# Scores of the second layer from block-diagonal keys, in one 128-row product of 512 columns for each query half

## What is computed

```python
def attention(q, k, v, mask):                 # for each batch and head
    scores = einsum('bqhd,bkhd->bhqk', q, k) * scale      # 256 x 256 for each head
    p = softmax(where(mask, -big, scores))
    return einsum('bhqk,bkhd->bqhd', p, v)
x = layernorm(x + attention(xWq, cWk, cWv) Wo)            # layer 0: "A", heads of 64
x = layernorm(x + attention(xWq, xWk, xWv) Wo)            # layer 1: "B", heads of 16
x = layernorm(x + attention(xWq, cWk, cWv) Wo)            # layer 1: "C", heads of 16
x = layernorm(x + relu(x W1) W2)
```

## Time and profile before

| | us |
|---|---|
| median of 3 runs | 1829.49 (1823.51 to 1831.89) |
| span of the profiled execution | 1832.3 |
| PE busy | 1728.2 (94% of the span) |
| PE weight loads | 1295.4 (71%) |
| DVE busy | 1280.9 (70%) |
| ACT busy | 1189.8 (65%) |
| POOL busy | 988.2 (54%) |
| mean busy share of the 16 DMA engines over the main queue's packets | 54.6% |
| granted clock of TensorE, mean | 0.986 |

### The profile page before, as it was taken

The page is one execution under the profiler, slowest core; times in us unless marked ns, Lnnn a source line. Parts: engine busy times, 40 slices in busy tenths (PEclk is TensorE's granted clock), DMA queues, the critical chain, the costliest instruction groups (busy, mean ns, idle before and its releaser), DMA issues.

```text
span 1832.3 us, 37274 instructions
## 1 busy us (share of the span) xinstructions
PE 1728.2 (94%) x11456; PEld 1295.4 (71%) x11456; DVE 1280.9 (70%) x4810; ACT 1189.8 (65%) x3985; POOL 988.2 (54%) x1030
## 2 busy tenths in 40 slices
PE   8698999999989999999999999999999999998887
PEld 6576777777767777777777777777776777775556
DVE  4265767776867867687776768677776867667763
ACT  4264676767666676776666677766767676566752
POOL 2244554647546464755646475554646555454742
PEclk9899999999999999999999999999999999999999
DMA  8421416575665857567585756758575675614110
GB/s 160 120 93 65 145 43 224 161 242 174 210 229 163 284 165 235 187 205 241 171 279 159 239 181 209 240 174 284 170 247 156 214 231 174 214 34 150 43 58 13
DMA packets 223171, 319.95 MB, mean 175 GB/s; under 512 B 31488, under 2 KB 192000, under 8 KB 214784
## 3 DMA queue, kind: packets, MB, share of 16 engines
q1 hardware_dynamic: 219856, 317.55, 54.6%
q10 hardware_dynamic: 3120, 0.01, 0.1%
HBM read 166.49 MB, written 151.00 MB: 173 GB/s over the span
## 4 chain that ended last, share of the span: by engine, by line
PE 77%; DMA 6%; DVE 6%; SPq 4%; ACT 4%; issue 2%; POOL 0%; POOLq 0%; DVEq 0%
PE ps_g L671 45%; PE ps_t L820 10%; PE ps_t L843 8%; PE ps_s L796 8%; PE ps_av L796 3%; DMA prob_b<-p_kept 3%; ACT prob L926 3%; PE ps_av L843 3%; DMA p_kept<-blocks 2%; DVE prob L1103 2%; PE ps_g L677 1%; SPq L584 1%; DVE res_ln L1079 1%; DMA x_tok<-x 1%; DVE prob_b L1134 1%
## 5 line engine op out<-in xcount | busy, mean ns | idle before, releaser
L1227 POOL TENSOR_TENSOR prob<-prob,recip 128x512 f32<-128x512 f32 x768 | 785.9, 1045 | 676.4 <-DVE recip L1113 671.5
L926 ACT ACTIVATE prob<-prob,ext 128x256 f32<-128x256 f32 x1536 | 757.2, 499 | 13.9 <-DVE ext L1103 13.4
L936 ACT ACTIVATE prob_t<-ps_t 128x512 f32<-128x512 f32 x384 | 226.4, 593 | 406.5 <-PE ps_t L820 405.6
L820 PE MATMUL ps_t<-ident,prob 128*128 128x128 f32 x1920 | 304.7, 284 | 7.0 <-DVE prob_b L1134 5.7
L926 ACT ACTIVATION_READ_ACCUMULATOR prob<-prob,ext 128x1 f32 x1536 | 295.0, 192 | 0.0
L820 PEld LDWEIGHTS ps_t<-ident,prob 128*128 128x128 f32 x1920 | 217.7, 142 | 92.7 <-issue 51.9
L1103 DVE CUSTOM_DVE_ANT_0 prob<-ps_s,mask_a 128x256 f32<-128x256 f32 x392 | 145.3, 421 | 87.3 <-PE ps_s L796 70.4
L1125 DVE STREAM_TRANSPOSE blocks<-prob 128x512 f32<-128x512 f32 x288 | 183.8, 676 | 2.3 <-POOL prob L1227 2.2
L1103 DVE CUSTOM_DVE_ANT_0 prob<-ps_s,zero 128x256 f32<-128x256 f32 x392 | 144.4, 418 | 49.8 <-PE ps_av L796 42.0
L1103 DVE CUSTOM_DVE_ANT_0 prob<-ps_s,mask_b 128x256 f32<-128x256 f32 x368 | 136.0, 417 | 24.1 <-PE ps_s L796 14.0
L796 PE MATMUL ps_s<-k_ctx,q 64*128 64x256 f32 x784 | 144.8, 402 | 5.8 <-DVE ext L1103 2.2
(11 more groups left out here) (122 smaller groups left out, 3022.6 us busy)
## 6 DMA issues: line engine op xcount, KB each, us to landing
p_kept<-blocks SPq DMA_DIRECT2D x576, 128.0 KB, 2.4
prob_b<-p_kept SPq DMA_DIRECT2D x144, 512.0 KB, 3.3
k_parts_C<-k_hl SPq DMA_DIRECT2D x64, 256.0 KB, 3.2
k_parts_B<-k_hl SPq DMA_DIRECT2D x64, 256.0 KB, 3.0
q_parts_B<-q_hl SPq DMA_DIRECT2D x64, 256.0 KB, 3.5
k_B<-k_parts_B SPq DMA_DIRECT2D x16, 1024.0 KB, 7.8
q_B<-q_parts_B SPq DMA_DIRECT2D x16, 1024.0 KB, 7.8
q_parts_C<-k_hl SPq DMA_DIRECT2D x64, 256.0 KB, 4.8
```

The source lines that it names most:

```text
L820: last = nc.tensor.transpose(two(ps_t[e])[:, kt, qt * P:(qt + 1) * P], src[:, e, qt, kt * P:(kt + 1) * P], ident[:, :])
L926: last = nc.scalar.activation(tile, tile, ACT.Exp, bias=ext[:, slot, e, t:t + 1], scale=-1.0, accum_out=sums[:, slot, e, t:t + 1])
L936: nc.scalar.activation(prob_t[:, e], two(ps_t[e]), ACT.Copy).then_inc(copied_second, 1)
L1227: nc.gpsimd.tensor_tensor(rows, rows, recip[:, slot, e].unsqueeze(2) .to_broadcast([P, TT, TOK]), ALU.mult).then_inc(normed[s], 1)
```

## The change

The keys of B and C get a second index: k4 is [128, 2, 8, 256] instead of [128, 8, 256]. Slice e holds head e's keys in rows 64e to 64e+63 and zeros in the other 64 rows, so the two slices side by side are block-diagonal. One product of 128 rows and 512 columns with the queries of half t gives both heads' scores of that half, in one PSUM bank. So there are two products for a pair instead of four, and a bank now holds a query half (both heads) instead of a head (both halves). DVE and ACT follow the new order for B and C; for A nothing is changed. The zeros are written once, by four memsets on DVE at the start, with a semaphore that PE waits for. The keys are read back with two DMAs of 64 partitions instead of one of 128, and the semaphore counts go from 16 to 32 with it. To make room in SBUF, the program's scratch for dynamic DMAs is set to 1024 bytes.

```diff
-        k4 = {s: sb("k4_" + s, [P, PAIRS, TOK], F32R) for s in "BC"}
+        k4 = {s: sb("k4_" + s, [P, 2, PAIRS, TOK], F32R) for s in "BC"}
@@ save_keys
-                    sp.wait_ge(spread_k["B"], count(b - 1, 16, 16))
+                    sp.wait_ge(spread_k["B"], count(b - 1, 32, 32))
@@ spread_keys
-                rows = "e a r c t -> (e a r) c t" if s == "B" else "b e a r c t -> (b e a r) c t"
-                sp.dma_start(k4[home][:, :, :].bitcast(F32), kept.rearrange(rows)).then_inc(spread_k[s], 16)
+                rows = "e a r c t -> e (a r) c t" if s == "B" else "b e a r c t -> e (b a r) c t"
+                for e in range(2):
+                    sp.dma_start(k4[home][HALF * e:HALF * (e + 1), e].bitcast(F32), kept.rearrange(rows)[e]
+                                 ).then_inc(spread_k[s], 16)
@@ scores
-                    pe.wait_ge(spread_k[s], count(b, 16, 16))
+                    pe.wait_ge(halves_cleared, 1)
+                    pe.wait_ge(spread_k[s], count(b, 32, 32))
-                    q, k = q4[home][:, place(p), :], k4[home][:, place(p), :]
+                    q, k = q4[home][:, place(p), :], k4[home][:, :, place(p), :]
+                if s != "A":
+                    for t in range(TT):
+                        nc.tensor.matmul(two(score_bank(body, step, t)), q[:, t * P:(t + 1) * P], k,
+                                         start=True, stop=True).then_inc(scored[s], 1)
+                    return
@@ exps
-                for e in range(2):
-                    act.wait_ge(masked[s], count(b, HEADS, 2 * p + e + 1))
-                    for t in range(TT):
+                for i in range(2):
+                    act.wait_ge(masked[s], count(b, HEADS, 2 * p + i + 1))
+                    for j in range(2):
+                        e, t = (i, j) if s == "A" else (j, i)
@@ start of the vector program
+            for s in "BC":
+                for e in range(2):
+                    last = nc.vector.memset(k4[s][HALF * e:HALF * (e + 1), 1 - e].bitcast(F32), 0.0)
+            last.then_inc(halves_cleared, 1)
@@ extremes (loops over i and j as in exps)
-                            out=prob[:, slot, e, t, :], in0=two(score_bank(body, step, e))[:, t, :], in1=mask,
+                            out=prob[:, slot, e, t, :], in0=two(score_bank(body, step, i))[:, j, :], in1=mask,
@@ kernel
-    nc = bacc.Bacc("TRN2", target_bir_lowering=False, num_devices=1)
+    nc = bacc.Bacc("TRN2", target_bir_lowering=False, num_devices=1, dynamic_dma_scratch_size=1024)
```

More of the change, by code:

```diff
@@ L410, in program @@
         own_ready = sem("own_ready")
+        halves_cleared = sem("halves_cleared")
         w_sorted, bias_sorted = sem("w_sorted"), sem("bias_sorted")
@@ L1095, in extremes @@
                     dve.wait_ge(mask_read, count(b, 1, 1))
-                for e in range(2):
-                    value = held(count(b, HEADS, 2 * p + e + 1))
+                for i in range(2):
+                    value = held(count(b, HEADS, 2 * p + i + 1))
                     dve.wait_ge(dve_const, 1)
                     dve.wait_ge(scored[s], value)
-                    for t in range(TT):
+                    for j in range(2):
+                        e, t = (i, j) if s == "A" else (j, i)
                         mask = {"A": mask_a[:, t, :], "B": mask_b[:, t, :],
```

## The result

| | before | changed |
|---|---|---|
| median, us | 1828.3 (6 runs) | 1841.6 (6 runs) |
| span of the profiled execution, us | 1832.3 | 1841.4 |
| ratio, 95% interval | | 1.008 (1.006 to 1.011) |

A forecast was written before the change was run, and what follows sets the result against it. PE was taken to bound the kernel; scores steps save 16.0 + 12.2 - 4.8 = 23.4 us, less 1 and 1 given back, 21 net, so the median goes from 1829.5 to 1808.5. Forecast 1798 to 1818 (0.70); eight in ten, 1794 to 1826.

The forecast's parts named there:

- What bounds the kernel: Whole kernel: PE, busy 94% of the span, is the time; its load-back waits of 20.0 and 14.9 us are small.
- rival 4: First score banks 0.21 us earlier also shorten waits for DVE and load-backs: at most 18 us more, 1791; chance 0.05.
- rival 3: Load-backs in full bodies swallow most gain: 6 us left, 1824; sign: wait for prob_b from 35 to some 50; chance 0.13.
- Emptying and exposed loads go away: Scores of B and C on PE: between transposes and a projection, a step falls from 0.95 to 0.76 us.
- rival 1: Borders of the scores: change of type still empties the array, only doubled streaming comes in, 54 us more, 1884; chance 0.08.
- rival 2: F32R scores products over 128 rows run at half speed, 0.432 us each: 87 us slower, 1917; chance 0.04.
- The size of a product: Scores of B and C: a product of 512 columns costs 2 x 0.107 = 0.214, taken as 0.216 us.
- the 23.4: Sum on PE over the 256 scores steps of B and C: 16.0 + 12.2 - 4.8 = 23.4 us less.
- The keys' two DMAs: SP's queue: 32 DMAs more, 0.33 to 1.04 us each, 11 to 33 us of a mostly waiting queue; same bytes.
- The prediction's own sign: PE's waits: the prediction is wrong if those for DVE or DMA move by more than 10 us.
- The memsets: Start, before DVE's first copy: at most 11.0 us, covered by waits, cost nothing; without that cover up to 6 us.
- The scratch size and the moved addresses: SBUF layout: they touch no work in the profile rows; costed at nothing.

The follow-up runs named there:

- the two comparisons: Changed products with one DMA for the keys: 1815.9 us against 1827.7 before; with C's queries read later in both kernels, 1811.9 us against 1823.0.

## Why the prediction was wrong, point by point

- **What bounds the kernel.** Right: PE, with the load-backs next. I had added the waits of the weight load and of the product, 20.0 and 14.9; they are mostly the same waits seen twice, so the 53.7 us of rival 4 and the 35 us of rival 3's sign are too large.
- **Emptying and exposed loads go away.** Right. Between transposes and a projection 0.95 became 0.79, where 0.76 was forecast; rival 1, in which the change of type drains, has no trace here. Nor has rival 2: a product takes 0.235 us and not 0.43. The sign named for it, starts 0.216 us apart, was the wrong one to look for, since the two starts of a step stand 0.31 to 0.34 us apart even so.
- **The size of a product.** Mis-sized. "Taken as 0.216" measured 0.23 to 0.24. I had the rate from a difference, with the exposed load in it, rounded down to half a float32 product. With 0.235, 0.02 us more for each of 512 products is 10 us off the 23.4, and 13 remain; by the measured steps 14 remain. The products brought 12 and 11 in the two comparisons. This alone would have left the kernel faster, at some 1818, inside the range.
- **The keys' two DMAs.** This is the step that failed: "the bytes are the same", with only SP's issue time costed. The bytes were the same and their time was not: 47 us more of all DMA engines, 25 us on the clock in the run with that part alone and 25 against the same products with one DMA. In the earlier trace rows I looked at the issue; the place to look was what each DMA covers. No row of the kernel before shows a 64-partition DMA that matters, and I should have bounded it: 31 read-backs of 1 MB at twice the time of a packet are some 2.5 us more of all engines each, 77 us in all (an estimate; 47 were measured), in a queue with one known late load-back behind it. (By the earlier trace rows, 16 and 15 read-backs, the DMAs more are 31 and not 32.)
- **Load-backs take the gain (rival 3).** Right in its place, with the wrong driver. It was not PE's speed: with one DMA for the keys the waits stay at 18.9 and 12.6 us. The slow keys made the load-backs late, and beyond rival 3's 1824: the waits grew from 35 to 73 us (counted twice, as there), where it had some 50. The prediction's own sign, a wait for DMA that moves by more than 10 us, was met. Its 17.5 us of gain in the full bodies are not what the terms give, 12 x 1.3 = 15.6.
- **More than the sum (rival 4).** No sign of it: PE's wait for DVE went from 18.8 to 17.9 us.
- **The memsets.** Inside their bounds, but hardly at nothing. They took 1.76 us each, DVE's first copy went from 6.86 to 10.59, and PE's restart behind the load of x_tok is at 67.72, before it was 68.35; the wait there fell from 12.06 to 6.69 us. This start varies by some 3 us from profile to profile, though. In the five profiles with about 7 us of memsets it is at 67.7 to 71.4 us, in the eight with 3.5 us or none at 65.5 to 68.4. The means are 69.2 and 66.5, so the memsets may have cost 2 to 3 us; no run tries them alone.

```profile
8.80 1.76 DVE L993 MEMSET k_C<- 64x2048 f32 x1 [0.47 <-issue]
10.59 0.69 DVE L1024 COPY x_t<-ps_g 128x512 f32<-128x512 f32 x1
...
67.72 1.08 PE L680 MATMUL ps_g<-ident,x_tok 128*128 128x128 f32 x4 [6.69 <-DMA x_tok<-x]
```

- **The scratch size and the moved addresses.** Not tried by themselves. The run with one DMA has them too and gains the 12 us that the measured steps leave, so nothing points to a cost there; its interval, 4 to 15 us of gain, would hide several us.

## What to carry to other kernels

A change of layout that turns one transfer over all partitions into two over halves is not neutral because the bytes are: cost it at twice the time of each packet (0.59 us for 0.31 here), and follow who stands behind it in the queue and in the issuing engine's order. If a layout needs two transfers, let each of them cover all of SBUF, for example by even and odd partitions; in a full-height product the order of the rows is free, as long as both operands follow it. If two runs are to tell one cause, look whether a memset or a wait at the start has changed with it. And a product's cost should be read from start to start with its load hidden; where the trace has no such case for a type, keep 10% in the range.

## What the runs showed of the hardware

- Two DMAs of 64 partitions for the keys cost 25 us in this kernel when they cover halves (1853.3, interval 16 to 41) and 4 us, in the noise, when they cover even and odd partitions (1831.8). Their 8 KB packets took 0.58 and 0.31 us.
- A load-back of 512 KB took 5.8 to 6.1 us from issue to landing with a read-back of 1 MB issued about 1.5 us before it, and 3.7 us with that read-back behind it.
- F32R products of 128 rows take 0.12 us for 256 columns and 0.235 for 512; a float32 instruction of 256 columns takes 0.216.
- Between float32 transposes, F32R products and float32 products, all of 128 rows and 128 columns of weights, there is no gap that compares with the 0.09 us at a change of tiles: 0.57 us from transpose to projection for 0.11 + 2 x 0.23.
- About 1 us after a wait of 3.51 us PE went to the 1.2 GHz level, with products 0.43 us apart instead of 0.216; in the full bodies of the changed kernel this happened 6 times, where the kernel before had it twice.
